# Sparse attention with a mixture of experts on one Trainium2 core: weighings of 256 queries in two parts, the next chunk's first scores ahead, expert weights in sixteen pieces

## What is computed

```python
h = _layernorm(x) * (1 + ca) + sa
routing_scores = sigmoid(sigmoid(relu(h @ r_w1.T + r_b1) @ r_w2.T + r_b2))
_, top_idx = top_k(rs_t, k_keep)               # 819 keys of each head
attn = einsum('bhqd,bhkd->bhqk', q, k) / sqrt(D)
sparse = where(keep[:, :, None, :], attn, NEG_INF)
w = softmax(sparse)
out = einsum('bhqk,bhkd->bhqd', w, v)
x = x + ga * out
h = _layernorm(x) * (1 + cb) + sb
x = x + gb * ffn(h)                            # h -> square(relu(h @ fc[e])) @ proj[e], e = argmax
```

## Time and profile before

| | |
|---|---|
| median of the runs | 523.1 us |
| the runs | 515.16, 523.27, 523.1 us |
| the profiled execution | 519.57 us |
| its span, first to last instruction | 517.7 us |
| mean granted clock of TensorE | 0.878 |
| busy: PE / DVE / ACT / POOL | 438.4 / 393.6 / 310.5 / 218.8 us |
| share of the chain that ended last: PE / DVE / DMA | 65 / 15 / 7% |

### The profile page before, as it was taken

One profiled execution on the slowest core, in us unless ns is written; L12 is line 12 of the kernel. 1 busy time (PEld: TensorE's weight loads), 2 busy tenths in 40 slices (PEclk: granted clock), 3 DMA queues, 4 the chain that ended last, 5 costly groups with the idle time before them and its releaser, 6 DMA issues.

```text
span 517.7 us, 9420 instructions
## 1 busy us (share of the span) xinstructions
PE 438.4 (85%) x3253; PEld 213.1 (41%) x3253; DVE 393.6 (76%) x1063; ACT 310.5 (60%) x457; POOL 218.8 (42%) x301
## 2 busy tenths in 40 slices
PE   3677557779999999999999999999999967089873
PEld 3342442223343343434433343334334327089872
DVE  8788948868898898689768967889889944836551
ACT  2435200357777778577657856777877863057662
POOL 2200274425346358348535824445100400077775
PEclk9878555599999999899879978999999995579998
DMA  8032600540100100010010010010000004022210
GB/s 246 3 122 68 158 7 4 184 150 4 35 4 5 36 5 5 4 36 3 5 35 4 4 35 5 5 31 8 3 2 2 22 1 143 0 74 57 66 30 21
DMA packets 20208, 21.11 MB, mean 41 GB/s; under 512 B 5741, under 2 KB 15793, under 8 KB 20161
## 3 DMA queue, kind: packets, MB, share of 16 engines
q1 hardware_dynamic: 14704, 16.12, 10.4%
q0 software_dynamic: 5168, 4.00, 3.9%
q10 hardware_dynamic: 288, 0.39, 0.2%
HBM read 14.41 MB, written 7.27 MB: 42 GB/s over the span
## 4 chain that ended last, share of the span: by engine, by line
PE 65%; DVE 15%; DMA 7%; issue 6%; POOL 3%; ACT 2%; SPq 0%; POOLq 0%; DVEq 0%; ACTq 0%
PE OP L1513 17%; PE ST L1497 12%; PE ST L1473 6%; DVE tile_max L1079 6%; PE SC L1451 6%; PE SC L1449 4%; PE ST L1645 3%; PE SC L1634 2%; DMA KV<-rows_dram,owner 2%; PE OP L1521 2%; DMA QS<-MT 2%; DVE PR L949 2%; DMA C<-in_const 1%; PE OP L1600 1%; PE ST L1403 1%
## 5 line engine op out<-in xcount | busy, mean ns | idle before, releaser
L1079 DVE TENSOR_REDUCE tile_max<-SC 128x1 f32<-128x410 f32 (+1 forms) x512 | 270.9, 576 | 55.5 <-PE SC L1449 51.2
L801 ACT ACTIVATE PR<-ST 128x1024 f32<-128x1024 f32 (+1 forms) x224 | 207.7, 961 | 52.0 <-PE ST L1497 51.3
L565 POOL DMA_INDIRECT G<-kv_dram,idx x104 | 107.4, 1033 | 169.6 <-ACT PR L801 93.6
L1497 PE MATMUL ST<-QS,KT 51*128 51x512 bf16 (+1 forms) x416 | 108.7, 397 | 4.5 <-DMA QS<-MT 4.2
L1513 PE MATMUL OP<-PR,VS 128*32 128x512 f32 x768 | 107.5, 633 | 0.4 <-ACT PR L801 0.4
L1449 PE MATMUL SC<-KT,QS 48*128 48x410 bf16 x256 | 79.3, 365 | 1.8 <-ACT KT L767 1.0
L1497 PEld LDWEIGHTS ST<-QS,KT 51*128 51x128 bf16 (+1 forms) x416 | 29.1, 96 | 54.2 <-issue 36.6
L1451 PE MATMUL SC<-KT,QS 48*128 48x409 bf16 x128 | 46.5, 364 | 3.6 <-DVE tile_max L1079 0.3
L696 POOL DMA_INDIRECT KV<-rows_dram,owner x23 | 24.7, 1073 | 50.5 <-DVE owner L1285 43.8
L1453 PE MATMUL SC<-KT,QS 48*128 48x358 bf16 x128 | 43.3, 338 | 0.7 <-DVE tile_max L1079 0.7
L1473 PE MATMUL ST<-C,OS 128*128 128x32 f32 x248 | 38.8, 281 | 0.2
(11 more groups left out here) (257 smaller groups left out, 533.2 us busy)
## 6 DMA issues: line engine op xcount, KB each, us to landing
kv_dram<-KV SPq DMA_DIRECT2D x4, 512.0 KB, 2.9
WE<-in_w_fc SPq DMA_DIRECT2D x1, 2048.0 KB, 9.9
WE<-in_w_proj SPq DMA_DIRECT2D x1, 2048.0 KB, 14.9
G<-kv_dram,idx POOLq DMA_INDIRECT x104, 2.4
q_parts_dram<-QP SPq DMA_DIRECT2D x3, 512.0 KB, 3.7
QS<-q_parts_dram SPq DMA_DIRECT2D x16, 96.0 KB
X<-in_x SPq DMA_DIRECT2D x4, 256.0 KB, 6.7
QS<-q_parts_dram SPq DMA_DIRECT2D x16, 64.0 KB
```

The lines of the kernel that those rows point to most:

```text
L565: pool.indirect_dma_start(G[:, i % 2, slot_of(s), :], None, kv_dram, bass.IndirectOffsetOnAxis(ap=idx[:, i, s:s + 1].bitcast(U32), axis=0) ...
L801: nc.scalar.activation(PR[:, k, 0:cols], ST[:, (KSTEPS * n + k) % 2, 0:cols], ACT.Exp, scale=float(D) ** -0.5).then_inc(exp_done, 1)
L1079: v.tensor_reduce(tile_max[:, n % 2, at_col:at_col + 1], bank(RING_AT["unit", u])[:, 0:410 - f], AX.X, ALU.max).then_inc(s_reduced, 1)
L1497: last = mm(ST[:, at_step % 2, 512 * e:512 * e + 512], KT[rows, i % 2, P * tile:P * tile + P], QS[rows, i % 2, CHUNK * c:CHUNK * (c + 1)], ...
```

## The change

Four things are changed in the attention, and one in SP's queue.

1. `weigh` gets an argument `half` and takes 256 of the 512 queries: four products of 256 columns. A chunk has six such parts in place of three weighings, and with the shared one seven counts of `pv_done` in place of four (`WEIGHS`); the waits of ACT and GpSimd are recounted.
2. The order of PE's queue in a chunk is written anew. The parts stand one to a step: (2, 4) for the queries 0 to 255, (5, 6) for the same, and the shared one with (5, 6) for the rest now stand in the first third of the next chunk; (0, 1) has its two parts around step 5; (2, 4) for the rest stands behind step 6. The two products of a step mostly stand side by side. Both turns of the result and the turn of the maxima follow each other.
3. The scores of step 0 of chunk n+1 stand ahead of the last unit of chunk n; those of chunk 0 stand ahead of the loop. The wait for the mask rows goes with them.
4. `LEAD` goes from 28 to 30, and the place of `turn_k` in the ring from 14 to 13.
5. The expert weights are loaded as 16 pieces of 256 KB, one behind the mask rows of each of the first 16 chunks.

```diff
@@ -44,17 +44,18 @@
 NQ = 4
+WEIGHS = 7
 CHUNK = L // NQ
 NCH = NP * NQ
 UPC = 16
-LEAD = 28
+LEAD = 30
 KSTEPS = 7
 RING = 3
 PACE = [0, 1, 3, 5, 7, 9, 11, 13, 15, 17, 19, 20, 22]
 GATHER_FROM = [0, 0, 2 * KSTEPS] + [KSTEPS * (NQ * (i - 2) + 1) + 5 for i in range(3, NP)]
 TURN_AT = {(2, 0): 1}
-TURN_AT.update({(NQ * (i - 1) + 1, 14): i for i in range(2, NP)})
+TURN_AT.update({(NQ * (i - 1) + 1, 13): i for i in range(2, NP)})
 AHEAD = 5
@@ -490,16 +491,19 @@
             sp.wait_ge(columns_ready, AHEAD)
-            for n, w_part in enumerate((w_fc, w_proj)):
-                sp.dma_start(WE[:, :, HD * n:HD * (n + 1)], w_part.rearrange("n p c -> p n c"))\
-                    .then_inc(we_in, 16)
+
+            def load_expert(piece):
+                at, half = piece // 2, piece % 2
+                sp.dma_start(WE[:, at, HD * half:HD * (half + 1)], (w_fc, w_proj)[half][at]).then_inc(we_in, 16)
+
             for n in range(NCH):
                 if n % NQ == 0 and 1 <= n // NQ < NP - 1:
                     sp.wait_ge(st_filled, KSTEPS * n)
                     load_q(n // NQ + 1)
                 if n + 1 < NCH:
                     m_rows(n + 1)
-
+                if n < 2 * NE:
+                    load_expert(n)
             for g in range(4):
...
@@ -796,19 +800,19 @@
                 if n >= 1:
-                    act.wait_ge(pv_done, 4 * (n - 1) + weighed)
+                    act.wait_ge(pv_done, WEIGHS * (n - 1) + weighed)
                 cols = 512 if k == 3 else 1024
                 nc.scalar.activation(PR[:, k, 0:cols], ST[:, (KSTEPS * n + k) % 2, 0:cols], ACT.Exp,
                                      scale=float(D) ** -0.5).then_inc(exp_done, 1)
             copy_mt(0)
             for n in range(NCH):
-                weights(n, 0, 1)
-                weights(n, 1, 1)
+                weights(n, 0, 2)
+                weights(n, 1, 2)
                 if n >= 1:
                     copy_o(n - 1)
-                weights(n, 2, 3)
-                weights(n, 3, 2)
+                weights(n, 2, 4)
+                weights(n, 3, 6)
                 if n >= 1:
@@ -819,11 +823,11 @@
                     copy_rows(LIST_BESIDE[n - 1])
-                weights(n, 4, 3)
-                weights(n, 5, 4)
+                weights(n, 4, 4)
+                weights(n, 5, 7)
                 if n % NQ == 1 and NQ < n < NQ * (NP - 1):
                     copy_kt(n // NQ + 1)
-                weights(n, 6, 4)
+                weights(n, 6, 7)
                 if n == 1:
...
@@ -1475,11 +1479,13 @@
                     last.then_inc(otr_done, 1)
-            def scores(n, k, e, first):
+            def scores(n, k, e, first=False, last=False):
                 i, c = n // NQ, n % NQ
                 at_step = KSTEPS * n + k
                 if first:
+                    if k == 0:
+                        pe.wait_ge(mrow, 32 * (n + 1))
                     if at_step >= 2:
@@ -1494,12 +1500,12 @@
                 tile = 6 if k == 3 else k - (k > 3)
-                last = mm(ST[:, at_step % 2, 512 * e:512 * e + 512], KT[rows, i % 2, P * tile:P * tile + P],
-                          QS[rows, i % 2, CHUNK * c:CHUNK * (c + 1)], start=True, stop=True)
-                if not first or k == 3:
-                    last.then_inc(st_filled, 1)
-
-            def weigh(n, steps_, first=False):
+                product = mm(ST[:, at_step % 2, 512 * e:512 * e + 512], KT[rows, i % 2, P * tile:P * tile + P],
+                             QS[rows, i % 2, CHUNK * c:CHUNK * (c + 1)], start=True, stop=True)
+                if last:
+                    product.then_inc(st_filled, 1)
+
+            def weigh(n, steps_, half, first=False):
                 i = n // NQ
@@ -1507,10 +1513,12 @@
                         pe.wait_ge(o_copied, n)
+                q0 = CHUNK // 2 * half
                 for g in range(4):
                     k, e = steps_[g // 2], g % 2
                     tile = 2 * (k - (k > 3)) + e
-                    last = mm(OP[32 * g:32 * g + 32, :], VS[:, i % 2, tile, :], PR[:, k, 512 * e:512 * e + 512],
+                    last = mm(OP[32 * g:32 * g + 32, q0:q0 + CHUNK // 2], VS[:, i % 2, tile, :],
+                              PR[:, k, 512 * e + q0:512 * e + q0 + CHUNK // 2],
                               start=first, stop=False, skip_group_check=True)
@@ -1545,6 +1553,8 @@
                 score_unit(u)
+            scores(0, 0, 0, first=True)
+            scores(0, 0, 1, last=True)
             for n in range(NCH):
@@ -1552,46 +1562,67 @@
                         score_unit(units.pop(0))
-                pe.wait_ge(mrow, 32 * (n + 1))
-                for k in range(KSTEPS):
-
-                    e = 1 - ORDER[units[0]][3] if units else 0
-                    if k == 3:
-                        scores(n, k, 0, True)
-                        unit()
-                        if n >= 1:
-                            turn_o(n - 1, (0, 1))
-                        unit()
-                        if n >= 1:
-                            turn_o(n - 1, (2, 3))
-                        if n in LIST_BESIDE:
-                            index_mm(LIST_BESIDE[n])
-                        if n - 1 in LIST_BESIDE:
-                            row_to_partition(LIST_BESIDE[n - 1])
-                        if n + 1 < NCH:
-                            turn_m(n + 1)
-                        continue
-                    scores(n, k, e, True)
-                    unit()
-                    scores(n, k, 1 - e, False)
-                    unit()
-                    if k == 1:
-                        if n >= 1:
-                            weigh(n - 1, (5, 6))
-                        unit()
-                    if k == 4:
-                        weigh(n, (0, 1), first=True)
-                        unit()
-                    if k == 5:
-                        weigh_shared(n)
-                        if n % NQ == 1 and NQ < n < NQ * (NP - 1):
-                            turn_k(n // NQ + 1)
-                    if k == 6 and n == 1:
-                        turn_k(1)
-                weigh(n, (2, 4))
+                if n >= 1:
+                    weigh(n - 1, (2, 4), 0)
                 unit()
+                scores(n, 1, 0, first=True)
+                scores(n, 1, 1, last=True)
+                unit()
+                if n >= 1:
+                    weigh(n - 1, (5, 6), 0)
+                unit()
+                unit()
+                if n >= 1:
+                    weigh_shared(n - 1)
+                if n >= 1:
+                    weigh(n - 1, (5, 6), 1)
+                unit()
+                unit()
+                scores(n, 2, 0, first=True)
+                scores(n, 2, 1, last=True)
+                scores(n, 3, 0, first=True, last=True)
+                unit()
+                if n >= 1:
+                    turn_o(n - 1, (0, 1))
+                if n >= 1:
+                    turn_o(n - 1, (2, 3))
+                if n in LIST_BESIDE:
+                    index_mm(LIST_BESIDE[n])
+                if n - 1 in LIST_BESIDE:
+                    row_to_partition(LIST_BESIDE[n - 1])
+                if n + 1 < NCH:
+                    turn_m(n + 1)
+                unit()
+                unit()
+                scores(n, 4, 1, first=True)
+                unit()
+                scores(n, 4, 0, last=True)
+                weigh(n, (0, 1), 1, first=True)
+                scores(n, 5, 0, first=True)
+                unit()
+                scores(n, 5, 1, last=True)
+                unit()
+                weigh(n, (0, 1), 0)
+                unit()
+                if n % NQ == 1 and NQ < n < NQ * (NP - 1):
+                    turn_k(n // NQ + 1)
+                scores(n, 6, 0, first=True)
+                scores(n, 6, 1, last=True)
+                unit()
+                weigh(n, (2, 4), 1)
+                unit()
+                if n + 1 < NCH:
+                    scores(n + 1, 0, 0, first=True)
+                    scores(n + 1, 0, 1, last=True)
+                unit()
+                if n == 1:
+                    turn_k(1)
                 assert not units
-            weigh(NCH - 1, (5, 6))
+
+            weigh(NCH - 1, (2, 4), 0)
+            weigh(NCH - 1, (5, 6), 0)
+            weigh_shared(NCH - 1)
+            weigh(NCH - 1, (5, 6), 1)
             turn_o(NCH - 1, (0, 1, 2, 3))
```

More of the change, by code:

```diff
@@ L606, in prep_v @@
                 if i >= 2:
-                    pool.wait_ge(pv_done, 4 * NQ * (i - 1))
+                    pool.wait_ge(pv_done, WEIGHS * NQ * (i - 1))
                 nc.gpsimd.tensor_copy(VS[:, b, 0:12:2, 0:D], G[:, b, 0:12:2, D:2 * D]).then_inc(v_step, 1)
@@ L781, in copy_o @@
             def copy_o(n):
-                act.wait_ge(pv_done, 4 * (n + 1))
+                act.wait_ge(pv_done, WEIGHS * (n + 1))
                 if n >= 1:
@@ L1286, in _ @@
             dve.wait_ge(tile_ready, 1)
-            dve.wait_ge(we_in, 32)
+            dve.wait_ge(we_in, 16 * 2 * NE)
```

## The result

The changed kernel takes 498.16 us, the median of four runs from 497.28 to 499.21; the kernel before took 523.18, the median of four from 515.16 to 523.76. The ratio is 0.961, with a 95% interval of 0.951 to 0.972. The profiled execution took 498.03 with a span of 496.1; before it was 519.57 with 517.7. The difference to be explained is 21.5 us, where 16.5 were forecast. (By the medians it is 25.0; the kernel before had medians of 519.5 to 521.2 beside the experiments, which makes it 21 to 23.)

A forecast was written before the change was run, and what follows sets the result against it. PE sets the chunk's time, 0.66 us of it waits for DVE. From 519.6, 28 chunks gain 12.0, the start gains 4.9 and the tail loses 0.4: 503 us, range 495 to 516.

The forecast's parts named there:

- The part of 256: Weighing of 256 queries on PE: 0.57 us, on a line between shared 0.36 and whole 1.00; bounds 0.50 and 0.68.
- rival (f): A weighing of 256 queries costs 0.68, the chunk 9.71, the whole 521 us; chance 0.04.
- PE's own work: TensorE's products, weighings, turns and array changes in an ordinary chunk, without waits: 8.91 us after, a rise of 0.17.
- 0.09 "left over": Ordinary chunk before: 9.40 us of summed work and waits against 9.49 measured; the remainder was assumed to stay in both kernels.
- Rival (b): PE's wait for maxima returns behind the turns, 0.45 us in each of 28 chunks, 516 us; chance 0.12.
- The chunks counted alike: Chunks 2 to 29, including those with an index list or turn of keys, each gain 0.43 us, together 12.0.
- rival (d): PE's shorter waits keep the clock at 2.4 GHz, gaining 4 to 12 us more, about 495; chance 0.10.
- The start: First two chunks: 9.5 and 9.6 us, 19.1 instead of 24.08 with the turn of keys, a gain of 4.9.
- rival (c): Mask rows for the next chunk's step 0 scores land 0.3 us late in each chunk, 511 us; chance 0.10.
- rival (e): Changes between half and full array let the clock fall in ordinary chunks, 517 to 548 us; chance 0.04.
- The sign that was wrong: PE's weight loads still waiting for maxima in every chunk would show the forecast wrong; no size given.
- (a): The forecast itself for the whole run: 503 us, own range 498 to 508; chance 0.60.

The follow-up runs named there:

- parts back to back: The kernel before with each weighing as two parts of 256 queries directly one behind the other, order otherwise as before: 523.82 us, ratio 1.002.
- first scores at the head: The changed kernel with the next chunk's step 0 scores back at that chunk's head, behind the first part there: 500.03 us, ratio 0.964.
- unit late: The changed kernel with the unit between the shared scores and the turns of the outputs moved behind those turns: 532.63 us, ratio 1.015.
- whole weighings: The changed kernel's order with weighings of 512 queries, each where one of its two parts stood: 537.24 us, ratio 1.031.

## Why the prediction was right, and where it was off

- **The bound.** Right. PE sets the chunk, and the waits for maxima came from a queue in which a weighing held PE for 1.00. Halving alone and order alone, as tried here, show that the cure needs both.
- **The part of 256.** Forecast 0.57, measured 0.57. The straight line between the shared weighing and the whole one was the right choice between 0.50 and 0.68; rival (f) falls.
- **PE's own work.** Forecast 8.91, measured 8.90, with PE busy for all of it. The turns came to 1.17 where 1.28 less 0.10 was summed, and the part behind the shared weighing to 0.43 where 0.47 was summed.
- **The ordinary chunk.** Forecast 9.05, measured 8.90. Two small terms failed. The 0.09 "left over" was carried into both kernels as if it were work; it is gone after, so it was no fixed work of PE's. Part of it may be a wait read too short: the second one, 0.22, is the idle time of a weight load, while by the prediction's own prices 921 columns from 346.04 and a way in let the last weighing start at 346.54, and it started at 346.80. What the rest was in the kernel before, no run shows. And the 0.05 of waits behind the turns did not come. Rival (b), the wait behind the turns, did not happen, but it was as close as the prediction's walk had it: one unit moved behind the turns brings it, at 0.58.
- **The chunks counted alike.** This step failed, in both directions. Five of the six chunks with a turn of the keys gained 0.16 instead of 0.43 (the first, whose turn waited for GpSimd before, 0.51): the sum took the turn's price from before, where it stood next to another full-array group, and did not ask what it would stand next to after. The nine chunks with or around an index list gained 8.4 instead of 3.9. Nine times 0.58 is 5.2; the other 3.2 go with 10.2 us less of low clock from the third chunk on (13.7 against 23.9). Chunks at full clock bear this out: three times 8.90, 11.18 and 9.16 after are 87.7, and three times 9.89, 9.75 and 11.44 before (the last from the kernel with parts back to back) are 93.2, so some 5.5 of the 8.4 are there without the clock. The rest is a part of rival (d), which had 0.10. In the changed kernel the clock fell at the sixteen products of an index list in two of three chunks, in the kernel before in all three, and the chain of waits has the parts behind it at 1.01:

```profile
203.81 1.98 PE ST L1407 x16
...
207.22 1.01 PE OP L1520 x8
...
209.11 1.01 PE OP L1520 x8
```

  In the kernel before it fell once more in the chunk that follows, in two of three; there a whole weighing takes 1.87, and a part takes 0.57 in the same place after:

```profile
269.67 1.87 PE OP L1513 x8
```

```profile
260.10 0.57 PE OP L1520 x8
```

  These second falls stand in the same two chunks (16 and 20) of all three kernels with chunks of 9.48 or 9.49, whose low time is 23.9 us each, and in none of the seven kernels with chunks of 9.02 or less, whose low time lies between 6.8 and 20.5. That the shorter waits cause it is likely from this, but no run changed it alone, and how often the clock falls in the index-list chunks themselves differs between profiles.
- **The start.** Forecast a gain of 4.9, measured 3.2. Neither a wait for mask rows nor GpSimd's preparation of the second pair's keys stands in the chain of the first two chunks any more, and in all PE waits for mask rows 0.8 instead of the 4.2 of the earlier trace rows (who waits for whom, us, times, longest):

```profile
PE ST L1503 <- DMA QS<-MT: 0.8, 2, 0.5
```

  But chunk 0 took 10.9 from its first scores, at 95.82, to the next chunk's, at 106.69, instead of 9.5. The step that failed is its price: 9.5 was taken between DVE's least, 8.2, and 10.55, and the measured time lies above both. The sum did not ask for the clock, which is low until 106.6 us, and the chunk's first parts read

```profile
101.99 1.01 PE OP L1520 x8
...
103.88 1.02 PE OP L1520 x8
```

  The kernel before was at low clock until 105.0 as well, so this could have been read from its trace.
- **The tail.** Forecast a loss of 0.4. From the last exponential to the last part's end it was 0.64 + 0.22 + 0.47 = 1.33 against one weighing of 1.11, a loss of 0.2. Chunk 31 as a whole, from its shared scores to the end of its last part, is even 0.2 shorter (6.15 against 6.35), chunk 30 is 0.07 longer (7.44 against 7.37), and the other 0.5 of the 0.7 lies behind the attention, whose program is unchanged.
- **The mask rows, rival (c).** It did not come: of the two waits for them that are left, one is the first chunk's and one the last chunk's, where no unit is left to cover them. With first scores at the head, where they have more time, the chunk is no shorter.
- **The clock, rival (e).** It did not come: the clock is 0.98 and 0.97 in the two stretches above, and what is missing lies in chunks with an index list. In the kernel before, too, the low time of the second stretch lies in chunks with an index list and right behind one, so the prediction's "the trace agrees for the second stretch" says more than the trace.
- **The sign that was wrong.** The prediction held that weight loads still waiting for maxima would speak against it. They still wait in every chunk, as the waits of the ordinary chunk above show (who waits for whom, us, times, longest):

```profile
PEld SC L1457 <- DVE tile_max L1083: 1.2, 3, 0.4
PEld SC L1453 <- DVE tile_max L1083: 1.0, 3, 0.4
```

  But PE streams other products meanwhile, and the matmuls wait for nothing in that stretch. So a weight load that waits need not be a loss; a chain with DVE in it is the better sign.
- **What had no term.** The two units ahead are worth 0.12 of the 0.58 a chunk, and the first scores ahead only 0.04.

Summed over the span: ordinary chunks with chunk 29 gave 2.1 more than forecast, the turns of the keys 1.3 less, the list chunks 4.5 more, the start 1.7 less, and what lies ahead and behind 1.4 more. That is 5.0 of the 5.0 by which the profiled execution, at 498.0, lies below 503. Misses of 3.0 one way and 8.0 the other stand behind it: that they partly cancel is luck, and the total lies at the lower end of the 498 to 508 that (a) was given, with part of (d) in it.

## What to carry to other kernels

Where an engine that feeds another one is held by one long step, look for a cut of that step and for work of the fed engine to put into the cut; neither helped alone here. After it, add up the feeder's own work with its pairings and its changes of array, and price each moved step by what it will stand next to. And price a stretch at the clock that the rows show there.

## What the runs showed of the hardware

- A change between half-array and full-array products and back costs TensorE 0.18 us in these kernels; two full-array groups side by side share it. That held for the shared scores beside the turns, and for a part, which takes 0.57 alone and 0.43 behind the shared weighing.
- TensorE's granted clock fell to 1.2 GHz away from the index lists, too: in the kernel with the unit late (a piece on DVE of 0.58 in each chunk's chain; mean clocks of 0.83 to 0.86 over its runs) and in the one with whole weighings (1.09; 0.86 to 0.87), against 0.88 for the changed kernel. The kernel before had pieces of 0.60, and its profile shows no low clock in an ordinary chunk; the one with parts back to back, with the same 0.60, shows it in one (10.79 instead of 9.49). The Trainium skill describes such falls in "TensorE: Matmul & The Clock Gate", section "A second HAM failure mode: psum-queue depth-cycling", for an engine that idles briefly between groups; the trace agrees for the first two kernels and hardly for the other two. So the length of such a piece alone does not decide, and what does stays open.
